# A decoder layer on one core: blocks of the scan rows placed by units, sums seven units behind, two orders in the last stage, and repeated transposes of the scan input

## The chip, the cores and the metric

The kernel runs on 1 core of one Trainium2 chip. The metric is the device time of one execution in microseconds, lower is better.

## What is computed

Input `x` (4 x 512 x 512) passes three sublayers, each followed by a layer norm of the sum:

```
x = layernorm(x + attention(x))     # 16 heads of 32, 4 kv heads; the attention axis has length 4 (x is read seq-first)
x = layernorm(x + ssm(ctx, z = x))  # in_proj, causal conv of 4 taps, silu -> u; x_proj -> dt, B, C; delta = softplus(...)
                                    # 16 states: h = h*exp(delta*A) + delta*u*B ; y = sum_n h_n*C_n + D*u ; y * silu(z)
x = layernorm(x + ffn(x))           # gate, up, down: weights are a 16-entry table looked up by index; silu(gate)*up
```

All arithmetic is float32 (in the feed-forward part as sums of split products).

## The kernel before

Five instruction streams are written out by hand, one for each engine (TensorE is PE, VectorE DVE, ScalarE ACT, GpSimd POOL, SyncE SP), and they meet at semaphores. Nothing schedules them: the order in the code is the order on the engine.

**Scan stage.** The four batch rows are called rows 0 to 3 of the program here (`b`). A row has 16 states `n`, a state 4 units `et` (tiles of 128 channels by 512 positions), so unit `k` runs from 0 to 255 and state `g` from 0 to 63. For each unit:

- ACT makes the input of four units at once (`scale_input`, L869, tile `scaled`, 3 buffers of states) and the decay of each (`decays`, L880, a ring of 8 units).
- PE transposes the input into one of 4 PSUM banks (`input_transposed`, L634, four 128x128 transposes). It waits until the scan four units back has freed the bank.
- DVE runs the recurrence (`scan`, L1170), 1.2 us a unit, into `state`, a ring of 4 states.
- POOL multiplies by C (`output_product`, L1419) and issues an accumulating DMA of each finished state to DRAM (`add_group`, L1430). A scan of state `g` waits until the DMA of `g-4` has landed.

Beside this the same engines do, a row ahead, the projections, convolution, softplus and attention of the next row. PE does these as jobs behind a transposed unit, placed by the tables `NEXT_AT`, `ALSO_AT`, `THEN_AT`, `ATT_AT` and `PROJ_AT` at (state, unit). Jobs take turns on the other 4 PSUM banks, so a job waits until the job four back has been read. The job kinds are `in` (L523), `kv` (L532), `q` (L538), `xp` (L546), `bt` (L553), `dt` (L559), `uT` (L565), `dT` (L572), `att` (L587) and `proj` (L596). ACT keeps their results at fixed states of its own loop, where it is two states ahead.

In the last 8 states of row 3 PE itself sums the states into four banks (`state_summed`, L643); before, the sum of unit `k` stands 12 units behind its transpose, since it is written `k // ET - 3`.

**Second norm.** POOL multiplies the outputs of rows 1 and 2 by their gates (`gate_row`, L1493) and raises variances to -1/2 (`stage2_rstd`, L1500). PE sums the residual (L649, L680, L682) and transposes (L692). ACT applies the norm (L958) and splits (`x2T_hi`, L969; its first call waits for `gate_row(2)`), and in between makes the leaves of the weight lookup (L988) that DVE selects among (L1198).

**Feed-forward.** 11 tiles `f`: PE multiplies four blocks of 512 tokens (`gate_up`, L707), each once `inner` of the tile before (DVE, L1249) has freed its banks. ACT makes `silus` (L1001), DVE `inner`. ACT's and DVE's work on weights (`leaves`, `select`) stands between them in `tile`. Then come the down products (L731) and the last norm.

## Time and profile before

| | |
|---|---|
| median of 3 runs | 993.14 us (989.9 to 993.56) |
| the profiled execution | 993.16 us, span 991.4 us |
| granted TensorE clock, mean | 0.909 of full |
| scan stage | first scan at 56.0 us, last at 538.5 us |
| second norm and first gate_up | 553.6 to about 632 us |
| feed-forward | to the end |

### The profile page before, as it was taken

The page shows a single profiled execution, that of the slowest core. Times are in us where ns is not written, and L with a number is a line of the kernel's source. Part 1 is how long each engine was busy: PE and PEld are TensorE (multiplying, and loading weights), DVE is VectorE, ACT ScalarE, POOL GpSimd, SP SyncE. Part 2 cuts the span into 40 slices and gives each one's busy share as a digit, 9 for nine tenths or more (in the row PEclk, how much of TensorE's full clock was granted, in tenths as well). Part 3 has the DMA queues.
Part 4 walks back from the last instruction along what each step waited for, and adds up shares of the span by engine and source line. Part 5 has one row for each costly group of instructions (what it writes and reads, how often), then busy time and mean ns, then how long its engine had stood idle before and what let it go on. Part 6 is the DMA issues. An engine that isn't in the chain of part 4 may idle for free.

```text
span 991.4 us, 11868 instructions
## 1 busy us (share of the span) xinstructions
PE 867.5 (88%) x3824; PEld 625.8 (63%) x3824; DVE 759.4 (77%) x1053; ACT 672.3 (68%) x994; POOL 497.1 (50%) x458
## 2 busy tenths in 40 slices
PE   7879798797888787786979888899999999899997
PEld 3447554476445564456545466787777778688885
DVE  3697899877998879986779566888888888355542
ACT  4598985789956899668696465677777776242321
POOL 0069867799767998669899631122111211001000
PEclk9789877989779897787989889999999999999999
DMA  7156989689985799968999222111111110223211
GB/s 247 51 162 166 224 162 210 139 219 250 211 212 118 203 240 214 221 125 205 208 278 280 88 96 85 43 50 57 42 42 42 48 58 21 74 85 107 85 64 53
DMA packets 49907, 135.98 MB, mean 137 GB/s; under 512 B 5364, under 2 KB 13684, under 8 KB 41156
## 3 DMA queue, kind: packets, MB, share of 16 engines
q0 software_dynamic: 8064, 58.72, 30.7%
q1 hardware_dynamic: 40432, 76.44, 23.0%
q10 hardware_dynamic: 1364, 0.25, 0.2%
q8 instruction: 23, 0.38, 0.2%
q14 instruction: 24, 0.20, 0.1%
HBM read 57.93 MB, written 78.51 MB: 138 GB/s over the span
## 4 chain that ended last, share of the span: by engine, by line
PE 27%; issue 23%; DVE 20%; ACT 18%; POOL 5%; DMA 5%; DVEq 1%; ACTq 0%; POOLq 0%; SPq 0%
PE banks L596 6%; PE banks L707 5%; ACT decay L880 5%; ACT scaled L869 5%; DVE state L1170 5%; PE banks L731 4%; DVE leaf L1198 3%; POOL state L1419 3%; PE banks L634 3%; PE banks L538 3%; DVE w_gu L1198 2%; ACT leaf L988 2%; DMA hT<-y_scratch 2%; DVE conv_in L1081 2%; DMA y_scratch<-state 1%
## 5 line engine op out<-in xcount | busy, mean ns | idle before, releaser
L1419 POOL TENSOR_TENSOR state<-state,crep 128x512 f32<-128x512 f32 x256 | 353.0, 1639 | 70.7 <-DVE state L1170 68.9
L1170 DVE TENSOR_TENSOR_SCAN state<-decay,banks 128x512 f32<-128x512 f32 x256 | 295.9, 1203 | 60.6 <-PE banks L634 45.4
L707 PE MATMUL banks<-x2T,wgu 128*128 128x512 f32 x1056 | 246.5, 393 | 4.9 <-DVE hT L1249 3.9
L634 PE MATMUL banks<-ident,scaled 128*128 128x128 f32 x1024 | 173.3, 311 | 72.3 <-DVE state L1170 53.4
L707 PEld LDWEIGHTS banks<-x2T,wgu 128*128 128x128 f32 x1056 | 197.9, 189 | 52.5 <-DVE hT L1249 11.1
L634 PEld LDWEIGHTS banks<-ident,scaled 128*128 128x128 f32 x1024 | 135.2, 160 | 145.7 <-DVE state L1170 64.9
L880 ACT ACTIVATE decay<-delta,negA 128x512 f32<-128x512 f32 x256 | 170.1, 724 | 77.4 <-DVE state L1170 77.0
L869 ACT ACTIVATE scaled<-duT,BT 128x512 f32<-128x512 f32 x256 | 163.8, 721 | 0.0
L988 ACT ACTIVATE leaf<-idx_sb,table,table_gap 128x1024 f32<-128x1024 uint8 (+1 forms) x132 | 129.5, 1023 | 6.7 <-DVE w_down L1198 3.2
L1198 DVE COPY_PREDICATED leaf<-idx_sb,leaf 128x1024 f32<-128x1024 uint8 (+1 forms) x88 | 94.1, 1070 | 6.4 <-issue 5.5
L1509 POOL TENSOR_TENSOR pool_wait_here<-minus_half 128x1 f32<-128x1 f32 x22 | 4.3, 194 | 179.7 <-DVE w_gu L1198 115.3
L731 PE MATMUL banks<-x2T 128*128 128x512 f32 (+1 forms) x264 | 83.2, 397 | 3.5 <-DVE x2T L1358 3.5
L731 PE MATMUL banks<-x2T,wgu 128*128 128x512 f32 (+1 forms) x264 | 81.4, 390 | 0.0
L1549 POOL TENSOR_TENSOR rstd<-vareps,minus_half 128x1 f32<-128x1 f32 x16 | 8.7, 542 | 140.7 <-DVE vareps L1377 140.7
L596 PE MATMUL banks<-wp,attT 128*128 128x512 f32 x128 | 62.6, 635 | 0.0
L731 PEld LDWEIGHTS banks<-x2T 128*128 128x128 f32 (+1 forms) x264 | 50.6, 192 | 14.7 <-issue 3.9
L1430 POOL DMA_DIRECT2D y_scratch<-state x52 | 57.1, 1098 | 3.2 <-DMA y_scratch<-state 3.2
L731 PEld LDWEIGHTS banks<-x2T,wgu 128*128 128x128 f32 (+1 forms) x264 | 49.6, 188 | 10.4
L1198 DVE COPY_PREDICATED w_gu<-idx_sb,leaf 128x1024 f32<-128x1024 uint8 x33 | 53.3, 1615 | 3.1 <-issue 2.7
L1069 ACT ACTIVATE leaf<-leaf,shift,rstd 128x512 f32<-128x512 f32 x16 | 13.1, 816 | 62.6 <-DVE shift L1380 62.6
L538 PE MATMUL banks<-wqkv,xT_sb 128*128 128x512 f32 x96 | 47.6, 644 | 2.7 <-DVE conv_in L1137 2.7
L1081 DVE SCALAR_TENSOR_TENSOR conv_in<-banks,ch,conv_in 128x511 f32<-128x511 f32 (+2 forms) x48 | 35.5, 743 | 12.7 <-ACT conv_in L777 11.6
(138 smaller groups left out, 1136.3 us busy)
## 6 DMA issues: line engine op xcount, KB each, us to landing
y_scratch<-state POOLq DMA_DIRECT2D x52, 1024.0 KB, 8.7
crep<-c_scratch SPq DMA_DIRECT2D x64, 256.0 KB, 5.4
idx_sb<-in_idx SPq DMA_DIRECT2D x11, 512.0 KB, 3.5
xT_sb<-in_xT SPq DMA_DIRECT2D x16, 256.0 KB, 4.7
y_scratch<-u SPq DMA_DIRECT2D x4, 1024.0 KB, 6.3
y_scratch<-state SPq DMA_DIRECT2D x4, 1024.0 KB, 6.3
leaf<-x_scratch SPq DMA_DIRECT2D x16, 256.0 KB, 2.7
out<-leaf SPq DMA_DIRECT2D x16, 256.0 KB, 2.0
```

The source lines that it names most:

```text
L538: last = mm(banks[:, bank, :], xT_sb[:, t, s, :], wqkv[:, t, 0:QT * P], start=t == 0, stop=t == HT - 1)
L596: last = mm(banks[:, bank, :], attT[:, s, t if s else 0, :], wp[:, t, :], start=t == 0, stop=t == QT - 1)
L634: last = nc.tensor.transpose(banks[:, k % NB, lc * LQ:(lc + 1) * LQ], scaled[:, g % SR, lc, et * P:(et + 1) * P], ident[:])
L707: last = mm(banks[:, 2 * tb + w, :], wgu[par][:, w, ws, t * P:(t + 1) * P], x2T[:, tb, xs, t, :], start=t == 0 and n == 0, stop=t == HT - ...
L731: last = mm(banks[:, bank, :], h[0:rows], w[0:rows, f, :], start=f == 0 and n == 0, stop=f == FT - 1 and n == 2)
L869: A(scaled[:, g % SR, lc, :], duT[m % 2][:, lc, :], ACT.Copy, scale=BT[:, m % 2, lc, n:n + 1])\
L880: A(decay[:, k % DR_RING, :], delta[m % 2][:, et, :], ACT.Exp, scale=negA[:, et, n:n + 1])\
L988: A(buffer(LEAF_ROLE[j], kind, parity), bit_of(0, kind, parity), ACT.Identity, bias=table[:, 2 * j:2 * j + 1], scale=table_gap[:, j:j + 1] ...
L1170: V.tensor_tensor_scan(state[:, g % GR, et, :], decay[:, k % DR_RING, :], banks[:, k % NB, :], 0.0, ALU.mult, ALU.add).then_inc(scan_ready, 1)
L1198: V.copy_predicated(buffer(kept, kind, parity), bit_of(bit, kind, parity), buffer(other, kind, parity)).then_inc(mux_ready, 1)
L1419: G.tensor_tensor(state[:, g % GR, et, :], state[:, g % GR, et, :], crep[:, g % CR, :], ALU.mult)\
L1430: pool.dma_start(total[:, b], group(g), accum_op=ALU.add).then_inc(group_sum(g)[0], 16)
```

## The change

The diff does five things: (1) att 2, and the kv jobs, move to other units of rows 0 to 2, on PE and where ACT keeps them; (2) the PE sums of row 3 stand 7 units behind instead of 12; (3) in rows 0 to 2, sixteen units in six states are transposed 2 to 4 times, to the same bank with the same result; (4) the first two silus of tile 0 and their inner products move ahead; (5) two `stage2_rstd` move ahead of `gate_row(2)`. SP's stream is the same.

```diff
+        SUM_LAG = 7
...
-                   (4, 2): ("kv", 0), (4, 3): ("kv", 1), (6, 0): ("kv", 2), (6, 1): ("kv", 3),
+                   (4, 3): ("kv", 0), (5, 1): ("kv", 1), (5, 3): ("kv", 2), (6, 2): ("kv", 3),
...
-        ATT_AT = {(3, 0): 3, (3, 1): 0, (4, 1): 2, (6, 0): 1}
+        ATT_AT = {(3, 0): 3, (3, 1): 0, (3, 2): 2, (6, 0): 1}
...
+                REPEATED = {(1, 3): 3, (2, 0): 3, (2, 1): 3, (8, 2): 2, (8, 3): 2, (9, 0): 2, (9, 1): 2, (9, 2): 4,
+                            (9, 3): 4, (10, 0): 2, (10, 2): 2, (10, 3): 2, (11, 0): 2, (11, 1): 2, (11, 2): 4, (11, 3): 4}
...
-                    for lc in range(S):
-                        last = nc.tensor.transpose(banks[:, k % NB, lc * LQ:(lc + 1) * LQ],
-                                                   scaled[:, g % SR, lc, et * P:(et + 1) * P], ident[:])
+                    times = REPEATED.get((g % DS, et), 1) if g < DS * (S - 1) else 1
+                    for _ in range(times):
+                        for lc in range(S):
+                            last = nc.tensor.transpose(banks[:, k % NB, lc * LQ:(lc + 1) * LQ],
+                                                       scaled[:, g % SR, lc, et * P:(et + 1) * P], ident[:])
...
-                    if k // ET - 3 >= G0:
-                        state_summed(k // ET - 3, k % ET)
-                for g in range(DS * S - 3, DS * S):
-                    for et in range(ET):
-                        state_summed(g, et)
+                    if k - SUM_LAG >= ET * G0:
+                        state_summed(*divmod(k - SUM_LAG, ET))
+                for k in range(UNITS - SUM_LAG, UNITS):
+                    state_summed(*divmod(k, ET))
...
-                        elif n == (4 if more else 3):
+                        elif n == 3:
                             keep_attT(b, 2)
-                        elif n == (5 if more else 4):
+                        elif n == 4 and not more:
                             keep_attT(b, 1)
...
                             elif n == 4:
                                 keep_bc(m)
+                            elif n == 5:
                                 keep_kv(c, 0)
                                 keep_kv(c, 1)
-                            elif n == 5:
                                 keep_kv(c, 2)
-                                keep_kv(c, 3)
+                                keep_attT(b, 1)
                                 keep_bt(m)
                             elif n == 6:
+                                keep_kv(c, 3)
                                 keep_uT(m)
...
                 x2T_hi(7)
+                silus(0, 0)
+                silus(0, 1)
                 high_part(1, 1)
...
                     leaves("down", f)
-                    silus(f, 0)
+                    if not isinstance(f, int):
+                        silus(f, 0)
...
                     select("down", f, then=("gate_up", f + 2))
-                    inner(f, 0)
+                    if not isinstance(f, int):
+                        inner(f, 0)
...
+                inner(0, 0)
+                inner(0, 1)
                 tile(0)
...
                 last_leaf(*FIRST)
+                stage2_rstd(0)
+                stage2_rstd(1)
                 gate_row(2)
-                for k in range(5):
+                for k in range(2, 5):
                     stage2_rstd(k)
```

(`silus(f, 1)` and `inner(f, 1)` are guarded in the same way.)

On PE, states 3 to 6 of row 1: L634 (L640 in the change) are the transposes of the scan input, 4 to a unit; prod_b is att 2, u is xp, xT_sb are kv jobs, prod_a is att 1, bc_dt is bt. Before:

```order
L634 MATMUL banks<-ident,scaled 128x128 x16
L587 MATMUL banks<-ident,prod_b 128x128 x12
L546 MATMUL banks<-u,xp_w 48x512 x4
L634 MATMUL banks<-ident,scaled 128x128 x4
L532 MATMUL banks<-wqkv,xT_sb 128x256 x4
L634 MATMUL banks<-ident,scaled 128x128 x4
L532 MATMUL banks<-wqkv,xT_sb 128x256 x4
L634 MATMUL banks<-ident,scaled 128x128 x20
L587 MATMUL banks<-ident,prod_a 128x128 x8
L532 MATMUL banks<-wqkv,xT_sb 128x256 x4
L634 MATMUL banks<-ident,scaled 128x128 x4
L553 MATMUL banks<-ident,bc_dt 128x16 x4
```

The same place in the change:

```order
L640 MATMUL banks<-ident,scaled 128x128 x4
L588 MATMUL banks<-ident,prod_b 128x128 x12
L640 MATMUL banks<-ident,scaled 128x128 x12
L547 MATMUL banks<-u,xp_w 48x512 x4
L640 MATMUL banks<-ident,scaled 128x128 x8
L533 MATMUL banks<-wqkv,xT_sb 128x256 x4
L640 MATMUL banks<-ident,scaled 128x128 x8
L533 MATMUL banks<-wqkv,xT_sb 128x256 x4
L640 MATMUL banks<-ident,scaled 128x128 x8
L533 MATMUL banks<-wqkv,xT_sb 128x256 x4
L640 MATMUL banks<-ident,scaled 128x128 x4
L588 MATMUL banks<-ident,prod_a 128x128 x8
```

Att 2 no longer stands straight before xp, and two units of transposes, not one, stand between the blocks.

On PE, states 8 to 12: bc_dt,dt_w are the four dt jobs, the last row is the first q job. Before:

```order
L559 MATMUL banks<-bc_dt,dt_w 128x512
L634 MATMUL banks<-ident,scaled 128x128 x28
L559 MATMUL banks<-bc_dt,dt_w 128x512
L634 MATMUL banks<-ident,scaled 128x128 x4
L559 MATMUL banks<-bc_dt,dt_w 128x512
L634 MATMUL banks<-ident,scaled 128x128 x28
L538 MATMUL banks<-wqkv,xT_sb 128x512 x4
```

In the change:

```order
L560 MATMUL banks<-bc_dt,dt_w 128x512
L640 MATMUL banks<-ident,scaled 128x128 x72
L560 MATMUL banks<-bc_dt,dt_w 128x512
L640 MATMUL banks<-ident,scaled 128x128 x4
L560 MATMUL banks<-bc_dt,dt_w 128x512
L640 MATMUL banks<-ident,scaled 128x128 x68
L539 MATMUL banks<-wqkv,xT_sb 128x512 x4
```

Seven units before the third dt job now take 18 rounds of four transposes, and the seven before q take 17.

On POOL after the scan: 128x2048 are `gate_row(1)` and `gate_row(2)`, rstd are `stage2_rstd`. Before:

```order
L1493 TENSOR_TENSOR rows_in<-rows_in,gate_in 128x2048
L1509 TENSOR_TENSOR pool_wait_here<-minus_half 128x1
L1510 TENSOR_SCALAR leaf<-idx_sb,table_gap,table 128x1024
L1493 TENSOR_TENSOR rows_in<-rows_in,gate_in 128x2048
L1500 TENSOR_TENSOR rstd<-vareps,minus_half 128x2 x5
```

In the change:

```order
L1507 TENSOR_TENSOR rows_in<-rows_in,gate_in 128x2048
L1523 TENSOR_TENSOR pool_wait_here<-minus_half 128x1
L1524 TENSOR_SCALAR leaf<-idx_sb,table_gap,table 128x1024
L1514 TENSOR_TENSOR rstd<-vareps,minus_half 128x2 x2
L1507 TENSOR_TENSOR rows_in<-rows_in,gate_in 128x2048
L1514 TENSOR_TENSOR rstd<-vareps,minus_half 128x2 x3
```

`gate_row(2)` now stands behind the first two rstd.

## Rows read from the trace of the kernel before

**Rows 1.** The page: busy time by engine.
```profile
PE 867.5 (88%) x3824; PEld 625.8 (63%) x3824; DVE 759.4 (77%) x1053; ACT 672.3 (68%) x994; POOL 497.1 (50%) x458
```
**Rows 2.** Busy time in two windows of row 1: us, busy (count) by engine, clock, DMA.
```profile
207.00:244.80 37.80, 33.65 (x202) 25.63 (x200) 27.66 (x25) 37.74 (x68) 36.21 (x33) 0.95 0.97 244
245.20:258.80 13.60, 10.30 (x35) 6.66 (x36) 13.60 (x17) 13.60 (x25) 12.00 (x12) 0.62 1.02 224
```
**Rows 3.** Waits of DVE from 207 to 245: who for whom, us, times, longest.
```profile
DVE state L1170 <- PE banks L634: 7.6, 5, 3.1
DVE state L1170 <- DMA y_scratch<-state: 2.5, 3, 1.1
```
**Rows 4.** Waits of ACT from 207 to 268 (its only one).
```profile
ACT decay L880 <- DVE state L1170: 0.4, 1, 0.4
```
**Rows 5.** Timeline of row 1, states 8 and 9: start, us, what.
```profile
243.78 1.10 ACT L824 ACTIVATE conv_in<-banks 128x512 f32<-128x512 f32 x2
244.06 1.22 DVE L1170 TENSOR_TENSOR_SCAN state<-decay,banks 128x512 f32<-128x512 f32 x1 [1.10 <-DMA y_scratch<-state]
245.20 1.26 DVE L1132 TENSOR_SCALAR delta<-banks 128x512 f32<-128x512 f32 x2
```
**Rows 6.** Timeline of DVE: the first product of q and keys, row 1.
```profile
267.40 2.29 DVE L1096 TENSOR_TENSOR prod_a<-banks,kv 128x2048 f32<-128x2048 f32 x1 [1.45 <-PE banks L538]
```
**Rows 7.** Timeline of PE: the first q job in rows 0, 1 and 2.
```profile
134.83 5.40 PE L538 MATMUL banks<-wqkv,xT_sb 128*128 128x512 f32 x8 [0.41 <-DVE conv_in L1137]
261.98 5.29 PE L538 MATMUL banks<-wqkv,xT_sb 128*128 128x512 f32 x8 [1.19 <-DVE conv_in L1137]
390.32 3.70 PE L538 MATMUL banks<-wqkv,xT_sb 128*128 128x512 f32 x8 [1.11 <-DVE conv_in L1137]
```
**Rows 8.** Timeline of PE: transposes at full clock, then states 10 and 11 of row 1.
```profile
219.98 1.91 PE L634 MATMUL banks<-ident,scaled 128*128 128x128 f32 x16
...
252.28 2.07 PE L559 MATMUL banks<-bc_dt,dt_w 17*128 17x512 f32 x2
...
254.28 4.82 PE L634 MATMUL banks<-ident,scaled 128*128 128x128 f32 x24
```
**Rows 9.** Windows of PE alone in row 1: us, busy (count), clock, DMA share, GB/s.
```profile
246.00:248.00 2.00, 0.64 (x4) 1.00 0.98 225
...
252.00:258.00 6.00, 6.00 (x22) 0.50 1.03 222
```
**Rows 10.** Row 3, transposes only: the PE timeline, then the window after it.
```profile
439.91 6.50 PE L634 MATMUL banks<-ident,scaled 128*128 128x128 f32 x24 [0.29 <-DVE state L1170]
...
447.00:449.00 2.00, 0.62 (x6) 1.00 1.06 213
```
**Rows 11.** Timeline of the second norm: POOL, ACT and DVE.
```profile
555.12 4.54 POOL L1493 TENSOR_TENSOR rows_in<-rows_in,gate_in 128x2048 f32<-128x2048 f32 x1
...
568.83 1.76 POOL L1500 TENSOR_TENSOR rstd<-vareps,minus_half 128x2 f32<-128x2 f32 x1 [2.47 <-DVE vareps L1230]
...
573.69 1.08 ACT L969 ACTIVATE x2T<-banks 128x512 fp32r<-128x512 f32 x2
...
575.94 1.29 DVE L1198 COPY_PREDICATED leaf<-idx_sb,leaf 128x1024 f32<-128x1024 uint8 x1 [2.00 <-issue]
```
**Rows 12.** Timeline of the first feed-forward tile: DVE and PE.
```profile
624.58 1.66 DVE L1198 COPY_PREDICATED w_down<-idx_sb,leaf 128x512 f32<-128x512 uint8 x1 [2.55 <-issue]
...
631.90 0.68 DVE L1249 TENSOR_TENSOR hT<-silu,banks 128x512 f32<-128x512 f32 x1
632.63 27.53 PE L707 MATMUL banks<-x2T,wgu 128*128 128x512 f32 x113 [2.54 <-DVE hT L1249]
```
**Rows 13.** Waits of PE from 640 to 860 (its only one).
```profile
PE banks L707 <- DVE hT L1249: 1.3, 6, 0.2
```
**Rows 14.** Timeline of PE and POOL near the end of the scans of row 3.
```profile
533.94 0.60 PE L634 MATMUL banks<-ident,scaled 128*128 128x128 f32 x4
...
528.95 4.31 POOL L1419 TENSOR_TENSOR state<-state,crep 128x512 f32<-128x512 f32 x3
```

More of the change, by code:

```diff
@@ L1036, in tile @@
                     leaves("down", f)
-                    silus(f, 0)
+                    if not isinstance(f, int):
+                        silus(f, 0)
                     leaves("gate_up", f + 2, early)
-                    silus(f, 1)
+                    if not isinstance(f, int):
+                        silus(f, 1)
                     leaves("gate_up", f + 2, late)
@@ L1335, in tile @@
                     select("down", f, then=("gate_up", f + 2))
-                    inner(f, 0)
+                    if not isinstance(f, int):
+                        inner(f, 0)
                     select("gate_up", f + 2, range(3), then=("down", f + 1))
-                    inner(f, 1)
+                    if not isinstance(f, int):
+                        inner(f, 1)
                     select("gate_up", f + 2, range(3, 6), then=("down", f + 1))
```

## The prediction

> **What bounds the kernel now.** I read the page first [rows 1]. PE is busy 88% of the span, DVE 77%, ACT 68%. These are averages over stages with different limits, so I then read windows and waits of each stage. Rows 0 to 2 of the program repeat one pattern; I work with row 1.
>
> In states 3 to 8 of row 1, from 207 to 244.8 us, DVE is idle 10 of 37.8 us [rows 2], of which 7.6 us wait for transposes, in five waits, and 2.5 us for accumulating DMAs [rows 3]. That looks like the prize of the first part of the change. But ACT is busy 37.74 of the same 37.80 us [rows 2] and has one wait of 0.4 us up to 268 [rows 4]. The stretch ends at the softplus of the next row on DVE, at 245.20. It needs ACT's logarithms, done at 243.78 + 1.10 = 244.88, and stands behind the scan of (9, 0), which started at 244.06 when a DMA landed and ended at 245.2 [rows 5]. So ACT and the DMAs both end here within 0.4 us of each other, and PE's lateness before is absorbed.
>
> From 245.2 to 258.8 DVE is busy all 13.60 us [rows 2]. The next place where DVE waits for PE is the product of q and keys: 1.45 us, for the first q job [rows 6]. That job took 5.40 and 5.29 us in rows 0 and 1, and 3.70 in row 2 [rows 7]: the same four products, partly at half clock in the first two. In row 2 DVE did not wait for it.
>
> Ahead of it PE worked 0.64 of 2 us at full clock [rows 9]; with that little work behind it the clock fell to 0.50, where it stood through 252 to 258 although PE was busy all 6 us [rows 9], two of them in the dt job, whose operand has 17 rows [rows 8].
>
> In the feed-forward part PE waits 1.3 us in 220 us, in six small waits for DVE [rows 13]: DVE and ACT with their table lookup set a period that PE just fills.
>
> **The change part by part.**
>
> *Blocks by units.* The work is the same, and so is ACT's in states 3 to 7 (att 2 is kept one state earlier, two kv one later, one kv two places later). PE's transposes of (4, 3), (5, 0) and (6, 1) come earlier, each no longer behind two blocks. Nothing that ends the stretch moves: ACT has no gap to close [rows 2, 4], and the DMA that (9, 0) waits for is not issued sooner by POOL, busy 36.21 of 37.80 us [rows 2]. Two of the jobs now wait for banks that ACT reads a state later, which takes back part of the lead. I take 0 for rows 0 to 2. Bounds: 0.5 us a row lost (one unit's transposes late by their own length, 0.48 [rows 8]), and 7.6 us a row won.
>
> *Repeats at (1, 3) to (2, 1).* Six extra rounds, each 1.91 / 4 = 0.48 us at full clock [rows 8], 2.9 us in all, while the scans there stand behind the convolution on DVE. They lie in PE's idle time: 0.
>
> *Repeats at (8, 2) to (11, 3).* 21 extra rounds a row. A round costs 0.48 us at full clock and 4.82 / 6 = 0.80 in a row of six that is mostly at half clock [rows 8]; at half clock alone I take 0.85. The first eleven extra rounds end before (10, 0), in idle time. They cannot keep the clock up through (10, 0) to (10, 1), since there is only the dt job and a wait of PE for DVE's softplus. So I expect half clock again at the third and fourth dt job, full clock a while into the repeats. Row 1: the last dt job ends at 254.35 before (252.28 + 2.07); with its start at full clock I take 0.65 less, 253.7. Scan (11, 0) needs (10, 2), (10, 3) and (11, 0), now six rounds: 253.7 + 6 x 0.85 = 258.8, against 257.7 before (DVE's window without a gap ends at 258.8 with this scan, 1.1 us), so DVE is about 1.0 us late there. All 16 rounds from (10, 2) to (11, 3) end at 253.7 + 6 x 0.85 + 10 x 0.45 = 263.3 (0.45 is the 0.48 without the tail of the last round), one more round for (12, 0) makes 263.75, then q at full clock takes 3.6: 267.35, less 0.4 as the clock rises within the first six. Before, q ended at 261.98 + 5.29 = 267.27. So DVE's product starts about 0.3 us earlier in rows 0 and 1, and in row 2, which had q at full clock, it is 1.0 us later. **Sum +0.4 us.** Bounds for the three rows: if no transpose is late and q runs at full clock, DVE gains its wait, 5.40 - 3.70 = 1.7 and 5.29 - 3.70 = 1.6, so -3.3; if the clock returns one step later (four more rounds at 0.85 instead of 0.45), +1.4, +1.4 and +2.9 us, +5.7.
>
> For the clock itself the trace has a stretch that holds only such transposes: 24 in 6.50 us at half clock in row 3, and behind it the granted clock is 1.00 with PE busy 0.62 of 2 us [rows 10]. So they do raise it. The Trainium skill (TensorE: Matmul & The Clock Gate, Part 4: PE-mode transpose) says that the full clock does not engage for transposes, since they do not count as PE work in the same way. By that rule the repeats would buy nothing; this trace disagrees, and the rule is a rival below.
>
> *Sums seven units behind.* PE does one sum behind each transpose at either distance, so its pace stays; only the tail behind the last transpose is shorter, and that lies under the last DMA. A sum now waits for POOL's product seven units back. At the transpose of (15, 0), 533.94, POOL had just finished (13, 3) at 528.95 + 4.31 = 533.26 [rows 14], and seven units back is (13, 1), done two products before. So no new wait: 0. If POOL fell behind by two more products of 1.4 us each, it would cost up to 2.8.
>
> *Norm order.* `gate_row(2)` ran from 555.12 to 559.66, and nothing waited behind it [rows 11]. It now starts after the second rstd, at 568.83 + 1.76 = 570.6, and ends 4.54 later, at 575.1. ACT's first split waits for it; it started at 573.69, so it is 1.4 us late. Behind it stands the last leaf, for which DVE waited until 575.94 [rows 11], and DVE, then PE, wait down the line. **+1.4 us.** Bounds: 0, if the chain has slack further on, and +2.4, if POOL and DVE slow each other.
>
> *First tile.* DVE idles 2.55 us at 624.58; two `inner` of 0.68 fit there, one at 631.90 [rows 12] stood directly ahead of the next select. PE idled 2.54 us at 632.63 for the first [rows 12] and starts at about 630.1 now. As DVE sets the period afterwards, the gain is what DVE gets ahead: 2 x 0.68 = 1.36, less 0.25 for leaves that come no sooner. **-1.1 us.** Bounds: 0 and -2.5 (PE's whole gap).
>
> Sum: 993.16 + 0.4 + 1.4 - 1.1 = 993.86, **993.9 us**. The profiled execution stands 0.02 us above the median, so this is the forecast for the median as well. A measurement of this kernel can tell about 0.5% (5 us) from no change, and 0.7 us is far inside.
>
> **The rivals.**
>
> *The clock stays up.* If the repeats keep it up far enough, DVE gains 3.3 us before q, and if the first projection block, which has q's shape, comes at full clock too, at most another 1.7 a row, 3.5 in two. With the norm order at 0 to 1.4 and the first tile at -1.1: 993.16 - 3.3 - 3.5 - 1.1 + 1.0 = 986.3. For it: q at full clock in row 2 let DVE run without a wait [rows 7]. Against it: PE's gap at (10, 0).
>
> *PE's lateness is the bound.* Then 3 x 7.6 us come back: 993.16 - 22.8 - 0.7 = 969.7. For it: the waits [rows 3]. Against it: ACT without a gap [rows 4].
>
> *Slower: the repeats stand in the way.* At (10, 2) to (11, 0) each scan needs a transpose that PE now does twice, at half clock. It decides once two rounds, 1.7 us, exceed the scan's 1.2 us [rows 5]. With the bounds above: 993.16 + 5.7 + 2.4 - 1.1 = 1000.2. For it: half clock all through this place [rows 9].
>
> *Transposes do not raise the clock.* Then 16 rounds at 0.85 end at 253.7 + 13.6 = 267.3, and q takes at least 5.3 more from 268.1: 6.1 us late in rows 0 and 1, 7.5 in row 2, in all 19.7, 1013. The rule of the Trainium skill cited above would have it so; against it stand [rows 10].
>
> **How the numbers follow.** The forecast has 0.54, the clock that stays up 0.22, PE as the bound 0.06, repeats in the way 0.14, transposes that do not count 0.04. Faster by over 0.5% (below 988.2): two thirds of the second, the third and a little of the first, 0.15 + 0.06 + 0.04 = 0.25. Slower by over 0.5% (above 998.1): 0.10 of the fourth, the fifth, and 0.03 of the first, 0.17. The rest, 0.58, is within. The likeliest case alone spans 990 to 997. The range goes from 985.5 (the clock that stays up) to 1000 (repeats in the way) and leaves the two ends out.
>
> **What would show it.** Right: ACT still without a gap in states 3 to 8 and scan (9, 0) still released by a DMA, with DVE's waits for PE smaller and those for DMAs larger. The granted clock at the third dt job 0.50, q at 3.6 us, and DVE's `prod_a` of row 1 within 0.5 us of where it stood behind scan (9, 0). `gate_row(2)` from about 570.6, DVE's wait of 2.0 us there at 3.4. PE without the gap of 2.54 us. Wrong: rows 0 to 2 shorter by more than 2 us each means that PE's transposes were the bound or the clock stayed up; scans of states 10 and 11 spaced at 1.7 us mean that the repeats stand in the way.

## The result and the profile after

| | before | changed |
|---|---|---|
| median of the runs | 993.17 us (9 runs, 989.9 to 995.5) | 996.75 us (9 runs, 995.2 to 997.8) |
| ratio to before | | 1.0041, 95% interval 1.0027 to 1.0055 |
| profiled execution: time, span | 993.16, 991.4 us | 997.77, 996.0 us |

The change costs 3.6 us of the median, 0.4%, a loss below the 0.5% that I called "no change". The profiled execution of the changed kernel lies 1 us above its median. Its engines, against [rows 1]:

```profile
PE 883.4 (89%) x4148; PEld 656.2 (66%) x4148; DVE 763.8 (77%) x1053; ACT 672.7 (68%) x994; POOL 499.0 (50%) x458
```

PE has 324 matmuls more, the repeats. DVE has as many instructions as before but is "busy" 4.4 us longer, and that is the first thing to look for. I cut the two executions at the same instructions. Up to the first scan of (3, 15) the changed kernel is 2.0 us late (536.6 against 534.6). From the fourth select of the second norm to the fifth it takes 4.0 us more; in the first feed-forward tile 0.8 us less (16.17 us from DVE's 21st select to its 29th before, 15.35 now).

**The second norm.** Timeline of DVE, the place of [rows 11] (start, us, instruction, the idle time ahead of it):

```profile
568.78 1.29 DVE L1234 BATCH_NORM_STATS2 stats<-banks 128x6 f32<-128x512 f32 x2
...
570.43 1.39 DVE L1208 COPY_PREDICATED w_gu<-idx_sb,leaf 128x1024 f32<-128x1024 uint8 x1
572.64 5.32 DVE L1208 COPY_PREDICATED leaf<-idx_sb,leaf 128x1024 f32<-128x1024 uint8 x1 [0.82 <-issue]
...
577.87 0.14 DVE L1245 SCALAR_TENSOR_TENSOR shift<-meanvar,rstd 128x2 f32<-128x2 f32 x1
...
581.62 1.29 DVE L1208 COPY_PREDICATED leaf<-idx_sb,leaf 128x1024 f32<-128x1024 uint8 x1 [2.00 <-issue]
```

and POOL beside it:

```profile
570.57 1.77 POOL L1514 TENSOR_TENSOR rstd<-vareps,minus_half 128x2 f32<-128x2 f32 x1 [2.45 <-DVE vareps L1240]
572.31 4.50 POOL L1507 TENSOR_TENSOR rows_in<-rows_in,gate_in 128x2048 f32<-128x2048 f32 x1
579.71 0.69 POOL L1514 TENSOR_TENSOR rstd<-vareps,minus_half 128x2 f32<-128x2 f32 x1 [2.89 <-DVE vareps L1240]
```

The select starts 0.33 us behind `gate_row(2)` and takes 5.32 us, where the same select took 1.36 before. It ends at 577.96: 1.15 us, about its own length, behind the end of POOL's product at 576.81. It shows no wait, because the time is inside the instruction. The shift, the statistics of the next half and ACT's `norm_apply` stand behind it.

The block goes both ways. POOL's `pow` (`rstd`) takes 0.69 us at 579.71, where DVE runs nothing beside it, and 1.77 us at 570.57, 0.14 us behind the start of a select; in the kernel before it took 1.76 us in that place too [rows 11].

**States 4 to 8 of row 1.** PE and ACT (the two engines' timelines, PE first):

```profile
225.72 0.60 PE L640 MATMUL banks<-ident,scaled 128*128 128x128 f32 x4
229.00 0.47 PE L554 MATMUL banks<-ident,bc_dt 16*128 16x16 f32 x4 [2.68 <-ACT kv L798]
...
228.58 0.91 ACT L798 ACTIVATE kv<-banks 128x256 f32<-128x256 f32 x3
...
235.09 0.72 ACT L885 ACTIVATE decay<-delta,negA 128x512 f32<-128x512 f32 x1 [0.73 <-DVE state L1180]
```

The `bt` job needs the bank of kv 0, which ACT now copies in state 5, so PE waits 2.7 us, in each of rows 0 to 2. DVE's waits over 207 to 244.8, against [rows 3]:

```profile
DVE state L1180 <- PE banks L640: 9.2, 5, 3.0
...
DVE state L1180 <- DMA y_scratch<-state: 0.2, 1, 0.2
```

DVE waits more for PE and less for DMAs, the reverse of what the spread suggests; even so scan (9, 0) starts at 244.12, against 244.06 in [rows 5], and a DMA still releases it. States 4 to 8 of row 0 took 34.0 us in place of 31.1, but they took 33.7 in run 2 and 33.6 in run 11, where the blocks stand at their old units, so that is not the blocks' doing.

**q.** The first q job in rows 0 to 2, against [rows 7], and DVE's first product in row 1, against [rows 6]:

```profile
135.38 3.67 PE L539 MATMUL banks<-wqkv,xT_sb 128*128 128x512 f32 x8
...
262.31 3.70 PE L539 MATMUL banks<-wqkv,xT_sb 128*128 128x512 f32 x8
...
391.23 3.60 PE L539 MATMUL banks<-wqkv,xT_sb 128*128 128x512 f32 x8
...
266.21 2.26 DVE L1106 TENSOR_TENSOR prod_a<-banks,kv 128x2048 f32<-128x2048 f32 x1
```

q comes at full clock in all three rows and DVE has no wait ahead of its product. PE alone in row 1, against [rows 9]:

```profile
252.00:258.00 6.00, 6.00 (x34) 5.07 (x32) 6.00 (x6) 6.00 (x11) 6.00 (x6) 0.72 1.02 214
```

PE was busy all 6 us both times; the mean granted clock was 0.50 before, 0.72 now. Row 2 paid for it:

```profile
379.42 2.07 PE L560 MATMUL banks<-bc_dt,dt_w 17*128 17x512 f32 x2
381.42 8.77 PE L640 MATMUL banks<-ident,scaled 128*128 128x128 f32 x57
...
383.43 1.22 DVE L1180 TENSOR_TENSOR_SCAN state<-decay,banks 128x512 f32<-128x512 f32 x1 [0.20 <-PE banks L640]
385.14 1.22 DVE L1180 TENSOR_TENSOR_SCAN state<-decay,banks 128x512 f32<-128x512 f32 x1 [0.49 <-PE banks L640]
386.69 1.22 DVE L1180 TENSOR_TENSOR_SCAN state<-decay,banks 128x512 f32<-128x512 f32 x1 [0.33 <-PE banks L640]
```

Here the last dt job came at half clock, and the scans of state 10 are spaced by 1.7 us, as the rival "repeats in the way" has it; the product then starts at 394.97, 0.8 us later than before, and 23.3 us behind scan (9, 0) in place of 21.8.

**The first tile.** DVE's gap of 2.55 us [rows 12] is one of 1.39; PE's of 2.54 us is gone, and a new one stands at the next tile:

```profile
629.98 1.66 DVE L1208 COPY_PREDICATED w_down<-idx_sb,leaf 128x512 f32<-128x512 uint8 x1 [1.39 <-issue]
...
648.15 4.31 PE L712 MATMUL banks<-x2T,wgu 128*128 128x512 f32 x11 [1.78 <-DVE hT L1259]
```

### The profile page after: what moved, and what is told of

It reads as the page before. It is cut to its first block, busy times and chain, and to the rows that moved or that the text cites. A ratio compares the mean times of both kernels' runs of the same rounds, so it can differ in the third digit from the quotient of the medians.

```text
span 996.0 us, 12516 instructions
## 1 busy us (share of the span) xinstructions
PE 883.4 (89%) x4148; PEld 656.2 (66%) x4148; DVE 763.8 (77%) x1053; ACT 672.7 (68%) x994; POOL 499.0 (50%) x458
## 3 DMA queue, kind: packets, MB, share of 16 engines
q1 hardware_dynamic: 40432, 76.44, 22.8%
## 4 chain that ended last, share of the span: by engine, by line
issue 19%; PE 15%; DVE 10%; POOL 5%; DMA 4%; ACT 3%; DVEq 1%; ACTq 0%; POOLq 0%; SPq 0%
PE banks L712 5%; PE banks L736 4%; DVE leaf L1208 3%; POOL state L1433 3%; PE banks L597 3%; DVE w_gu L1208 2%; ACT leaf L994 2%; DMA hT<-y_scratch 2%; DMA y_scratch<-state 1%; DMA y_scratch<-y_scratch 1%; DVE idx_sb L1192 1%; PE banks L685 1%; POOL rstd L1565 1%; DVE w_down L1208 1%; ACT w_down L994 1%
## 5 line engine op out<-in xcount | busy, mean ns | idle before, releaser
L640 PE MATMUL banks<-ident,scaled 128*128 128x128 f32 x1348 | 196.6, 294 | 49.4 <-DVE state L1180 46.0
L640 PEld LDWEIGHTS banks<-ident,scaled 128*128 128x128 f32 x1348 | 167.0, 152 | 110.4 <-DVE state L1180 48.0
L1208 DVE COPY_PREDICATED leaf<-idx_sb,leaf 128x1024 f32<-128x1024 uint8 (+1 forms) x88 | 98.4, 1119 | 7.1 <-issue 6.3
L597 PEld LDWEIGHTS banks<-wp,attT 128*128 128x128 f32 x128 | 26.0, 214 | 27.2 <-issue 27.2
```

What stands on the lines that cost most here:

```text
L597: last = mm(banks[:, bank, :], attT[:, s, t if s else 0, :], wp[:, t, :], start=t == 0, stop=t == QT - 1)
L640: last = nc.tensor.transpose(banks[:, k % NB, lc * LQ:(lc + 1) * LQ], scaled[:, g % SR, lc, et * P:(et + 1) * P], ident[:])
L1208: V.copy_predicated(buffer(kept, kind, parity), bit_of(bit, kind, parity), buffer(other, kind, parity)).then_inc(mux_ready, 1)
```

## The experiments

Every ratio is to the kernel before on the same chip, with its 95% interval. Theory A at the start: the norm order costs 4.0 us through the select, and the rest of the change is small in sum.

**1. Norm order undone** in the changed kernel.

```diff
-                stage2_rstd(0)
-                stage2_rstd(1)
                 gate_row(2)
-                for k in range(2, 5):
+                for k in range(5):
```

> The changed kernel with the norm order undone: POOL runs gate_row(2) ahead of the first stage2_rstd, as before. Theory A (from the two traces): in the changed kernel the select of a leaf on DVE that starts at 572.64, 0.3 us after gate_row(2), took 5.32 us in place of 1.36, so the norm order costs 4.0 us and more than explains the 3.6 us between the medians; then this kernel takes 996.75 - 4.0 = 992.8 us, and the select is 1.4 us long again. Rival, my forecast's term: only ACT's split waited, 1.4 us; then 995.4 us. Rival: the delay is absorbed further on and the scan stage holds the loss: 996.7 us.

Measured: 993.05 us, ratio 0.9996 (0.9983 to 1.0009), 0.45% below the changed kernel. The select:

```profile
571.54 1.36 DVE L1208 COPY_PREDICATED leaf<-idx_sb,leaf 128x1024 f32<-128x1024 uint8 x1 [0.83 <-issue]
```

One POOL instruction moved is the whole loss. Theory A holds, my 1.4 us does not (run 5 shows where it went).

**2. Blocks at their old units** (both tables and ACT's copies as before, the rest changed).

> The changed kernel with the blocks at their old units (att 2 at (4, 1), kv at (4, 2), (4, 3), (6, 0), (6, 1), ACT's copies as before). Forecast's term: 0, so 996.7 us. Theory A: the spread costs, since the job bt now waits 2.7 us for ACT's copy of kv 0, which comes a state later, and this makes DVE and then ACT idle (0.6 to 0.7 us a row): against the trace of before scan (9, 0) is 2.9, -0.1 and 0.8 us late in rows 0 to 2, so about 3 us come back: 994 us. Rival: the spread gains (row 1 became 1.7 us shorter), and undoing it loses 1 to 3 us: 998 to 1000 us.

Measured: 997.17 us, 1.0035 (1.0016 to 1.0054), 0.06% below the changed kernel; the two intervals together leave about 2.4 us to either side. The bank wait of 2.7 us costs nothing that the medians show, and the rest of the spread wins nothing that they show: the 3 us that I read from three row lengths were not there.

**3. No repeats.**

```diff
-                REPEATED = {(1, 3): 3, (2, 0): 3, ...
+                REPEATED = {}
```

> The changed kernel without repeated transposes. Forecast's term: the repeats cost 0.4 us, so 996.3 us. Theory A (from the traces): with the repeats q comes at full clock in rows 0 and 1 and DVE's wait of 1.45 to 1.56 us is gone, while in row 2 the scans of (10, x) are about 1.5 us late; net gain 1.7 us, so without them 998.4 us, with a q of 5.3 us in at least two rows. Rival (transposes do not raise the clock): q's clock in the changed kernel comes from another alignment; then q stays at 3.7 us without the repeats and this kernel is faster, by 1 us or more, 995 us.

Measured: 997.38 us, 1.0036 (1.0019 to 1.0054), the same as the changed kernel. In the profile q is slow again in rows 0 and 1:

```profile
134.39 5.08 PE L539 MATMUL banks<-wqkv,xT_sb 128*128 128x512 f32 x8 [0.41 <-DVE conv_in L1146]
...
262.56 5.40 PE L539 MATMUL banks<-wqkv,xT_sb 128*128 128x512 f32 x8 [0.52 <-DVE conv_in L1146]
```

So the repeats do raise the clock ahead of q, without a gain in the time. Runs 10 to 12 take that further.

**4. Sums twelve units behind.**

> The changed kernel with the sums twelve units behind (three states) as before. Forecast's term: 0, so 996.7 us. Rival: the sums at seven units wait for POOL (two waits of 0.5 us on PE in row 3 of the changed kernel) and lengthen row 3, where (3, 11) is 0.8 us later than its row's start says: then 995.9 us. Rival: the shorter tail behind the last transpose was worth 1 us and is lost: 997.7 us.

Measured: 995.87 us, 1.0023 (1.0009 to 1.0037), 0.18% below the changed kernel, which these intervals don't separate. Run 8 asks again.

**5. `gate_row(2)` in four instructions**, at its new place.

```diff
+                    if b == 2:
+                        for t in range(S - 1):
+                            G.tensor_tensor(yb[b][:, t], yb[b][:, t], gate[b][:, t], ALU.mult)
+                        G.tensor_tensor(yb[b][:, S - 1], yb[b][:, S - 1], gate[b][:, S - 1], ALU.mult).then_inc(pool_gated, 1)
+                        return
```

> The changed kernel with gate_row(2) at its new place, but written as four instructions of 128x512 (about 1.1 us each) in place of one of 128x2048 (4.50 us). Theory A: DVE's select and POOL's product of two SBUF operands can't run together; whichever starts second waits until the other instruction has ended. The select that starts 0.3 us behind gate_row(2) then waits only for the rest of the first part, 0.8 us, and takes 2.2 us instead of 5.32; POOL's second part waits for the select in turn. Of the 4.0 us that the norm order costs, 3.2 come back: 996.75 - 3.2 = 993.6 us. Rival: POOL issues its parts back to back and the select still waits for all four: 5.3 us and 996.7 us. Rival: the engines share bandwidth, and both are slowed for as long as POOL works: again about 5 us, 996.7 us.

Measured: 995.09 us, 1.0016 (1.0003 to 1.0029), 0.25% below the changed kernel. Timelines of DVE, POOL and ACT:

```profile
569.74 2.16 DVE L1208 COPY_PREDICATED leaf<-idx_sb,leaf 128x1024 f32<-128x1024 uint8 x1 [0.83 <-issue]
...
571.77 1.24 DVE L1245 SCALAR_TENSOR_TENSOR shift<-meanvar,rstd 128x2 f32<-128x2 f32 x1
572.93 1.28 DVE L1234 BATCH_NORM_STATS2 stats<-banks 128x6 f32<-128x512 f32 x2
...
574.47 1.01 DVE L1240 TENSOR_SCALAR vareps<-meanvar 128x2 f32<-128x2 f32 x1
...
569.39 4.82 POOL L1509 TENSOR_TENSOR rows_in<-rows_in,gate_in 128x512 f32<-128x512 f32 x3
574.17 1.28 POOL L1510 TENSOR_TENSOR rows_in<-rows_in,gate_in 128x512 f32<-128x512 f32 x1
...
573.04 1.45 ACT L964 ACTIVATE rows_in<-banks,shift,rstd 128x512 f32<-128x512 f32 x2 [3.35 <-DVE shift L1245]
575.48 1.08 ACT L975 ACTIVATE x2T<-banks 128x512 fp32r<-128x512 f32 x2 [0.99 <-POOL rows_in L1510]
```

The select takes 2.16 us, as Theory A had it. Of POOL's first three parts, 4.82 us together, the second takes 2.37 us and the others 1.27: the two engines take turns by instruction. That speaks against shared bandwidth and against parts issued back to back. The mend is worth less than 3.2 us, for two reasons that I missed. The next DVE instructions are blocked in turn, the shift (1.24 us, 0.14 otherwise) and `vareps` (1.01, 0.17 otherwise), though they touch two elements a partition. The statistics, which read PSUM, run undisturbed beside POOL (1.28 us for two). And ACT's split, once the select no longer holds it up for longer, waits 0.99 us for the last part of `gate_row(2)`: this is the path of my forecast. From the fourth select to the fifth it is 8.0 us here, 9.0 in the changed kernel and 5.0 before, so 1.0 us of the 4.0 comes back there, and 0.5 us is left of it at the end (behind run 12); the rest of the 0.25% is within the interval.

The same path can be read in the changed kernel. Before, the split started 2.8 us behind the start of the fourth select (573.69 and 570.91); with a select of the old length it would have been ready at 575.4 there, and `gate_row(2)` ended at 576.81. That is 1.4 us, my term, hidden behind the 4.0 us of the blocked select.

The Trainium skill (SBUF — State Buffer, "SBUF: two separate sides") has this as a rule: VectorE and GpSimd share a pair of SBUF ports as an exclusive lock, held for a whole instruction; a VectorE instruction with two SBUF inputs meets a GpSimd one that reads SBUF, and the later one fully blocks. The traces agree, with 5.32 and 2.16 us against 1.36 for the select, and 1.77 against 0.69 us for POOL's `pow` where the select came first.

**6. The first tile alone**, on the kernel before.

> The kernel before, with the first tile's edit alone (two silus and two inner ahead of the first select). Forecast's term: -1.1 us against before. Theory from the two traces: the gap of 2.54 us on PE goes, and one of 1.78 us comes at the next tile, where h_ready is late, so 0.8 us are left: -0.8 us, 0.9992 of before. Rival: nothing is left, since DVE sets the period afterwards and its own order there is the same work: 1.0000. Rival: all of PE's gap is won, -2.5 us, 0.9975.

Measured: 992.75 us, 0.9991 (0.9977 to 1.0005). From DVE's 21st select to its 29th 15.34 us, 16.17 before: 0.8 us, and 15.3 to 15.4 in every profile with the edit.

**7. Copies of kv 0 and kv 1 a state earlier**, on run 1's kernel.

```diff
                             elif n == 4:
                                 keep_bc(m)
-                            elif n == 5:
                                 keep_kv(c, 0)
                                 keep_kv(c, 1)
+                            elif n == 5:
                                 keep_kv(c, 2)
```

> The changed kernel with the norm order undone, and ACT's copies of kv 0 and kv 1 in state 4, as before the change, and not in state 5. Theory B: in the changed kernel PE waits 2.7 us at the job bt for ACT's copy of kv 0 in each of rows 0 to 2, DVE is late for it at three scans of state 6 and ACT once by 0.6 to 0.7 us. With the copy a state earlier this wait is gone; states 4 to 6 get shorter by about 2 us each, but ACT, which is busy all through them, sets the end of the stretch, so a row gains only ACT's 0.65 us: 0.9996 less 2 us, 0.9976 of before. Rival: PE's lateness is the bound after all and all of DVE's waits of state 6, some 5 us a row, come back: 0.985. Rival: nothing, the accumulating DMAs set the end: 0.9996.

Measured: 997.86 us, 1.0047 (1.0030 to 1.0063): 0.5% slower than run 1, where I expected 0.2% faster. No theory had it. The wait had moved:

```profile
237.26 0.66 PE L566 MATMUL banks<-ident,u 128*128 128x128 f32 x4 [3.25 <-ACT kv L798]
237.75 1.54 PE L640 MATMUL banks<-ident,scaled 128*128 128x128 f32 x8
239.22 2.07 PE L560 MATMUL banks<-bc_dt,dt_w 17*128 17x512 f32 x2
241.22 1.11 PE L640 MATMUL banks<-ident,scaled 128*128 128x128 f32 x4
242.26 2.07 PE L560 MATMUL banks<-bc_dt,dt_w 17*128 17x512 f32 x2
...
246.27 1.22 DVE L1180 TENSOR_TENSOR_SCAN state<-decay,banks 128x512 f32<-128x512 f32 x1 [2.68 <-PE banks L640]
```

A `uT` job now waits for the copy of kv 3, which ACT makes after all of the state's scales and decays. The dt jobs behind it come at half clock, and DVE waits at a scan of state 8, with the softplus directly behind it. States 4 to 8 of row 1 take 36.2 us, against 33.1 in the changed kernel.

**8. The same, sums twelve units behind.**

> As e7_mend_kv0, and the sums twelve units behind as before the change. If the run with the sums alone undone (0.18% below the changed kernel, its interval touching none) measured an effect of the sums, this one is 1 to 1.8 us below e7_mend_kv0; if that was scatter, it is the same within 1 us. Theory A says scatter: in the two traces row 3 differs between them by less than the clock's alignment makes.

Measured: 998.67 us, 1.0054 (1.0036 to 1.0072), against 1.0047 in run 7. The sums' distance is worth nothing that can be seen; run 4's 0.18% was scatter.

**9. Kv 3 earlier as well.**

```diff
                                 keep_bt(m)
+                                keep_kv(c, 3)
                             elif n == 6:
-                                keep_kv(c, 3)
                                 keep_uT(m)
```

> The changed kernel with the norm order undone, ACT's copies of kv 0 and kv 1 in state 4, and that of kv 3 at the end of state 5 and not ahead of uT in state 6. In e7_mend_kv0 the wait of PE only moved: its third uT job waited 3.25 us for the copy of kv 3, the dt jobs behind it came at half clock, and DVE waited 2.7 us at a scan of state 8, which stands directly ahead of the softplus; states 4 to 8 of row 1 took 36.2 us there, against 33.1 in the changed kernel and 33.2 before. Theory C: a wait of PE in state 6 is absorbed (ACT and the DMAs set the end), one in states 7 and 8 is not. With both copies early enough PE waits nowhere in states 5 to 8; the five states take what ACT needs, 33.0 us: 5 us come back against e7, and against the kernel with the norm order alone undone (0.9996 of before) 0 to 2 us are gained: 0.998. Rival: the dt jobs come at half clock for another reason, and it stays at e7's 1.0047. Rival: PE's lateness was the bound, and states 4 to 8 fall below 31 us: 0.99.

Measured: 992.86 us, 0.9997 (0.9985 to 1.0009): the 5 us of run 7 come back, and nothing beyond run 1. The two waits, each 2.7 to 3.3 us on PE, are the same kind of thing; the one at `bt` costs nothing that these intervals show, the one at `uT` 1.7 us a row. But states 4 to 8 of row 1 did not fall to 33.0 us; in this profile they took 34.8:

```profile
231.71 0.60 PE L640 MATMUL banks<-ident,scaled 128*128 128x128 f32 x4
233.78 0.63 PE L640 MATMUL banks<-ident,scaled 128*128 128x128 f32 x4 [1.46 <-DVE state L1180]
235.17 2.07 PE L560 MATMUL banks<-bc_dt,dt_w 17*128 17x512 f32 x2 [0.77 <-ACT duT L837]
```

PE, now ahead of the others, idles for them, 2.2 to 2.3 us ahead of the first dt job in each row, where it idled 1.0 to 1.2 us before the change. In rows 1 and 2 the jobs behind came at half clock, the first of row 2 in part, in row 0 at full. So the lead of PE turned into idle time, and in two rows of three the low clock that followed took the lead back; that the idle time is what lowered the clock fits these rows, but no run tests it alone.

**10. Fewer repeats**, on run 9's kernel: (10, 0), (10, 2), (10, 3) and (11, 0) once.

```diff
-                            (9, 3): 4, (10, 0): 2, (10, 2): 2, (10, 3): 2, (11, 0): 2, (11, 1): 2, (11, 2): 4, (11, 3): 4}
+                            (9, 3): 4, (11, 1): 2, (11, 2): 4, (11, 3): 4}
```

> As e9_mend_kv0_and_kv3, with the transposes of (10, 0), (10, 2), (10, 3) and (11, 0) done once. Theory A: in some rows (row 2 of the changed kernel) state 10 takes 5.75 us in place of 4.45, since each scan there waits for a transpose that PE does twice at half clock; with these once this can't happen, and the repeats at (11, 1) to (11, 3) still bring the clock up for q. Where it happened in one row of three: -0.4 to -0.6 us against e9; at most -1.5. Rival: without them the clock rises later, and q comes at half clock in part again: q at 4.5 us or more, +1 us or more.

Measured: 989.45 us (6 runs), 0.9968 (0.9955 to 0.9981): faster than before, and 0.3% below run 9, more than I expected. q stays at 3.70 us in all three rows. Its profiled execution is the odd one of the six: 994.27 us, where the other five lie between 988.9 and 989.9. So no trace shows where the 3.4 us went. My theory covers a part at most: of the nine profiles with the four entries (the changed kernel, runs 1, 2, 4, 5, 7, 8, 9, 11) seven have a row with a state 10 of 5.7 us or more, and none of the five without them; that is 1.3 us a profile on average, and run 9's own profile has none. The other 2 us stay open.

**11. Repeats alone**, on the kernel before.

> The kernel before, with the repeated transposes alone. Forecast's term: +0.4 us. Theory A: q at full clock (3.7 us) in rows 0 to 2, where DVE then has no wait of 1.5 us, and one row in three loses 1.5 us at state 10: -1.5 to -3 us, 0.998 of before. Rival (transposes do not raise the clock, or the repeats stand in the way): q at 5.3 us or more, and +6 us or more, 1.006.

Measured: 992.72 us, 1.0005 (0.9989 to 1.0021). q takes 3.70, 3.60 and 3.60 us, yet nothing is gained: rows 1 and 2 of this profile have the late scans of state 10. Row 2:

```profile
382.81 1.22 DVE L1175 TENSOR_TENSOR_SCAN state<-decay,banks 128x512 f32<-128x512 f32 x1 [0.66 <-PE banks L639]
384.52 1.22 DVE L1175 TENSOR_TENSOR_SCAN state<-decay,banks 128x512 f32<-128x512 f32 x1 [0.49 <-PE banks L639]
386.28 1.22 DVE L1175 TENSOR_TENSOR_SCAN state<-decay,banks 128x512 f32<-128x512 f32 x1 [0.54 <-PE banks L639]
```

**12. Fewer repeats, blocks at their old units, norm order undone.** What is left of the change: these repeats, the sums and the first tile.

> As e10_fewer_repeats, but with the blocks at their old units, as in the kernel before: what is left of the change are the fewer repeats, the sums seven units behind and the first tile. Theory: the blocks by units bring nothing even when no bank is late, since ACT and the DMAs set the end of states 4 to 8 (33.2 us in row 1 before, 33.8 in the profiled execution of e10); then this kernel is within 1.5 us of e10's 0.9968. Rival: it is the mended spread that made e10 faster than before; then this one returns to that kernel's time, 0.9995 or more.

Measured: 989.14 us, 0.9945 (0.9923 to 0.9967), the lowest ratio, faster than both kernels; its interval overlaps that of run 10. So the spread, mended or not, brings nothing that can be seen. Its row 2, where the dt job came at half clock just as in the changed kernel:

```profile
379.42 2.07 PE L560 MATMUL banks<-bc_dt,dt_w 17*128 17x512 f32 x2
...
377.11 8.99 DVE L1179 TENSOR_TENSOR_SCAN state<-decay,banks 128x512 f32<-128x512 f32 x8
...
389.39 3.60 PE L539 MATMUL banks<-wqkv,xT_sb 128*128 128x512 f32 x8
```

Eight scans without a gap (1.12 us each), and q at full clock behind them: the four transposes on the path are done once, and the repeats after them still bring the clock up in time.

**What the repeats give.** From the start of scan (9, 0) to DVE's first product of q and keys, the three rows of a profile added up:

| repeats | us |
|---|---|
| none: before, runs 3, 6 | 70.0, 68.9, 69.9 |
| sixteen entries: changed kernel, runs 1, 2, 4, 5, 7, 8, 9, 11 | 67.2, 66.1, 67.8, 68.0, 67.1, 66.9, 67.5, 65.7, 69.4 |
| twelve entries: runs 10, 12 | 65.4, 66.0 |

With twelve, every row is at 21.8 to 22.1 us, and no row of any profile is shorter than that. Twelve entries save 3.9 us here against none, by the means, and the time falls with them (0.9968 and 0.9945, against 0.9991 in run 6). Sixteen save 2.3 us, which neither run 3 nor run 11 shows in the time (run 11's own profile saves 0.6 us); where the rest is lost was not found.

**How far one execution can be trusted.** The changed kernel, run 1 and run 5 have the same code up to the second norm, yet their profiled executions start scan (3, 15) at 536.6, 535.5 and 533.9 us. What differs from one to the next, as far as I read them, is where the granted clock falls and rises, and with it one or two us of a row. From scan (3, 15) to the end the picture is cleaner:

| span less the start of scan (3, 15), first tile changed | us |
|---|---|
| norm order changed, one instruction: changed kernel, runs 2, 3, 4 | 459.4, 458.9, 459.3, 459.0 |
| the same in four instructions: run 5 | 458.7 |
| norm order as before: runs 1, 6, 7, 8, 9, 10, 12 | 455.9, 456.0, 455.3, 455.8, 455.4, 455.6, 455.0 |

459.15 less 455.57, the means of the outer groups, is 3.6 us for the norm order, as much as the difference of the medians. The two kernels without the first tile's edit show that this cut scatters as well: 456.7 before and 454.1 in run 11, with the same code there. The scatter lies ahead of the second norm's fourth select. From its start to the end the groups are 423.3 to 423.7, 422.9, and 419.6 to 420.2 us, and the two others 420.4 and 420.1: again 3.6 us for the norm order, 0.5 given back by run 5, and 0.5 us for the first tile.

## Why the prediction came out as it did

I forecast 993.9 us and "no change" with 0.58; 996.75 us lies in the range and under the 0.5%. The sum was 2.9 us short, and one term explains most of it. That the verdict held is partly luck: the largest loss came by a mechanism that the forecast had only in a bound, too low and not in its sum, and it was small enough for the range. Of the signs that I named, scan (9, 0) released by a DMA, q at 3.6 us, the place of `gate_row(2)` and the closed gap of 2.54 us held. DVE's waits for PE and DMAs, ACT without a gap, the clock at the third dt job, the place of `prod_a` and the wait of 3.4 us (it stayed at 2.00) did not.

- **Blocks, 0: right within about 2.4 us, its reasons half right.** That ACT and the DMAs set the end of the stretch, and not PE, held: a wait of 2.7 us more on PE moved scan (9, 0) of row 1 by 0.06 us, and undoing the part gave nothing (run 2). I had said that two jobs would wait for banks that ACT reads later, and named no price; it was 2.7 us of PE at `bt`. My signs for it were wrong: DVE's waits for PE rose, and ACT got gaps of 0.7 and 0.4 us. And "PE's lateness is absorbed" holds for state 6 only; run 7 put the same lateness into states 7 and 8 and lost 5 us.
- **Repeats, +0.4: right in sum** (run 11 +0.5 us with 1.6 to either side, run 3 the same within its interval), **wrong in its parts, and so right by luck.** The clock: q at 3.6 to 3.7 us in every row, as forecast, but the third dt job came at full clock too, in every row, and the fourth in rows 0 and 1 (from 246 to 248 PE was busy 1.55 us, with the repeats, in place of 0.64 [rows 9]); the clock fell later, and in row 1 the product started 22.1 us behind scan (9, 0) in place of 23.3, 1.2 us sooner and not 0.3; row 0 came 3.0 us sooner and row 2, with the loss at state 10, 1.5 us later. For the three rows together I had +0.4 us there, and this profile has -2.8; what takes it back was not found. State 14 of row 0 lasted 11.6 us in place of 10.2, but 11.5 without any repeat (run 3) and 10.3 with all of them (run 11), so it is not that. The mechanism of my rival "repeats in the way" is at work in some rows. Without its four entries the kernel is 0.3% faster (run 10 against run 9), of which late scans explain a part. That rival's bound was added up wrong as well: with four rounds at 0.85 in place of 0.45 its terms give 1.3, 1.3 and 2.6 us, 5.2 and not 5.7. The eleventh extra round, which I had end before (10, 0), is that of (10, 0) itself.
- **Sums, 0: right** (runs 7 and 8).
- **Norm order, +1.4: the term that failed,** +3.6 to +4.0 measured, with a bound of 2.4 that left it out. I counted who waits on a semaphore for the moved instruction (ACT's split) and not who runs beside it. The path that I counted exists and would have cost 1.4 us (run 5), but the blocked select holds up the same split for longer. I had named "if POOL and DVE slow each other" and priced it by no row, though the kernel before has the row. The selects into `w_gu` there, shortest, median and longest in ns:

```profile
L1198 DVE COPY_PREDICATED w_gu<-idx_sb,leaf x33: 1356/1397/2261, 564.5 to 825.0; 128x1024 f32<-128x1024 uint8 x33
```

Nine of them take 2.2 us in place of 1.4, one in each of nine feed-forward tiles, and each started 0.2 us behind a POOL instruction of 1.2 us (the last leaf). There it can cost little, as PE waits only 1.3 us in 220 [rows 13]. "A select waits for what is left of POOL's instruction" would have given, for one of 4.54 us that starts 0.3 us ahead, 4.2 us.
- **First tile, -1.1: right in kind,** -0.8 measured over the tile in the trace of run 6, of which 0.5 us is left at the end; its ratio alone (0.9991, 0.9977 to 1.0005) does not tell it from nothing. PE's gap came back at the next tile, with 1.78 us.
- **Rivals.** "The clock stays up" was half of what happened (q), without the time; with twelve entries (runs 10 and 12) the time came as well, 2.3 and 4.6 us below run 6 by the ratios, about this rival's 3.3. "Transposes do not raise the clock" is refuted: in rows 0 and 1 q takes 3.6 to 3.7 us with the repeats and 5.1 to 5.4 without. PE as the bound, 22.8 us, is refuted by runs 2 and 9: taking away PE's wait of 2.7 us at `bt` gained nothing.

## What to carry to other kernels

Before an instruction is moved on one engine, look at what the other engines run at its new place, and at the longest instance of each instruction there against its median: a block inside an instruction shows in no list of waits. Extra work that only serves the clock belongs beside idle time; each piece of it that someone waits for is paid at the low clock, and leaving out four of the sixteen entries turned no gain into 0.3%. Where executions of the same code differ by 2 us or more in a stage, a term of 1 us read from one trace is no evidence; cut the traces where they are quiet, or measure the part alone.

## What the runs showed that I had not expected

A POOL product of two SBUF operands stopped DVE's select for what was left of its length (5.32 us for 1.36), and even a DVE instruction on two elements a partition for 0.8 to 1.1 us; statistics read from PSUM were not touched. Who starts second waits: a `pow` on 128x2 started 0.14 us behind a select took POOL 1.77 us and left the select at 1.39, and it takes 0.69 us where no DVE instruction runs. The kernel before has this on its way too: its `pow` at 581.60 started 0.14 us behind a select and took 1.73 us, and DVE's next shift waited 0.55 us for it. Two equal waits on PE, 2.7 us at `bt` and 3.25 us at `uT` one state later, were worth nothing and 1.7 us a row; the second was followed by half clock in the jobs on the path. Where PE was given a lead (run 9), idle time and the same half clock followed in two rows of three.
